# Graph attention with layer norm on one core: other row groups, the rows of p made earlier, the bins turned to a row earlier, squares on ScalarE

## The reference, cut to what matters

```
Wh, We = x @ W, ent @ W
p, q = Wh @ a1, We @ a2
e = leaky_relu(p[:, None] + q[None, :], 0.2)
e = where(adj > 0, e, -9e15)
h = softmax(e, axis=1) @ ent + x
x = x + elu(h)
out = (x - mean(x)) / sqrt(var(x) + 1e-5)      # over the 64 features
```

## Time and profile before

| | us |
|---|---|
| median of 3 runs | 375.44 (375.23 to 376.32) |
| profiled execution | 377.46 |
| its span | 375.4 |
| DVE busy | 308.4 (82%) |
| PE busy | 305.7 (81%) |
| ACT busy | 264.4 (70%) |
| POOL busy | 47.2 (13%) |

### The profile page before, as it was taken

One profiled execution on the slowest core, in us unless ns is written; L12 is line 12 of the kernel. 1 busy time (PEld: TensorE's weight loads), 2 busy tenths in 40 slices (PEclk: granted clock), 3 DMA queues, 4 the chain that ended last, 5 costly groups with the idle time before them and its releaser, 6 DMA issues.

```text
span 375.4 us, 9071 instructions
## 1 busy us (share of the span) xinstructions
PE 305.7 (81%) x3920; PEld 163.2 (43%) x3920; DVE 308.4 (82%) x436; ACT 264.4 (70%) x263; POOL 47.2 (13%) x54
## 2 busy tenths in 40 slices
PE   1379599997879999996999979879997767957750
PEld 0356466665545554552545435335442313412220
DVE  1894586863797999569899996799999999999955
ACT  1163299897588989589999975799876568646530
POOL 5012111110101001400100041000000500000201
PEclk9999879998989999998999989999999999999995
DMA  7999999999977940999665009940000000000000
GB/s 151 251 206 174 186 200 161 205 207 208 188 119 115 151 74 2 144 208 209 103 91 81 0 3 168 205 72 0 2 2 2 2 28 3 3 0 2 0 30 22
DMA packets 35240, 37.32 MB, mean 99 GB/s; under 512 B 832, under 2 KB 34432, under 8 KB 35200
## 3 DMA queue, kind: packets, MB, share of 16 engines
q0 software_dynamic: 33408, 33.56, 56.3%
q1 hardware_dynamic: 1792, 3.18, 3.0%
HBM read 69.24 MB, written 1.05 MB: 187 GB/s over the span
## 4 chain that ended last, share of the span: by engine, by line
PE 35%; DVE 27%; issue 23%; ACT 11%; DMA 2%; POOL 1%; POOLq 0%; DVEq 0%; SPq 0%; ACTq 0%
PE acc L744 13%; PE pairs L693 10%; DVE xm L522 8%; DVE wts L530 7%; PE acc L747 6%; ACT mask L315 5%; ACT wts L329 3%; PE hist L709 3%; DMA ent_sb<-ent_blocks_dram 2%; DVE y L563 1%; PE misc L668 1%; ACT drow L340 1%; DVE ent_part L615 1%; PE misc L724 1%; POOL rstd L272 1%
## 5 line engine op out<-in xcount | busy, mean ns | idle before, releaser
L329 ACT ACTIVATE wts<-wts,q_bias 128x768 f32<-128x768 f32 (+2 forms) x160 | 152.1, 976 | 56.1 <-DVE wts L530 55.9
L744 PE MATMUL acc<-wts,ent_sb 128*32 128x384 f32 (+2 forms) x1280 | 152.5, 525 | 28.3 <-ACT wts L329 19.4
L530 DVE SCALAR_TENSOR_TENSOR wts<-pb,q_bend,xm 128x768 f32<-128x768 f32 (+2 forms) x160 | 167.5, 1070 | 8.2 <-PE acc L747 7.7
L315 ACT ACTIVATE mask<-pairs 128x2048 bf16<-128x2048 bf16 (+2 forms) x67 | 104.3, 1559 | 35.8 <-PE pairs L693 35.5
L747 PE MATMUL acc<-wts,onesf 128*32 128x256 f32 (+1 forms) x1152 | 93.2, 362 | 0.0
L522 DVE TENSOR_TENSOR xm<-mask,drow 128x1536 bf16<-128x1536 bf16 (+2 forms) x80 | 80.8, 1010 | 9.9 <-ACT drow L340 9.9
L693 PE MATMUL pairs<-ident,raw 128*128 128x128 bf16 x1024 | 79.5, 235 | 1.8 <-ACT mask L315 0.9
L693 PEld LDWEIGHTS pairs<-ident,raw 128*128 128x128 bf16 x1024 | 65.2, 106 | 27.9 <-issue 27.5
L747 PEld LDWEIGHTS acc<-wts,onesf 128*32 128x32 f32 x1152 | 41.7, 112 | 71.3 <-issue 66.0
L744 PEld LDWEIGHTS acc<-wts,ent_sb 128*32 128x32 f32 x1280 | 34.7, 109 | 57.7 <-ACT wts L329 43.3
L266 POOL DMA_DIRECT2D raw<-adj_dram x40 | 33.4, 836 | 153.9 <-PE pairs L693 151.3
(11 more groups left out here) (99 smaller groups left out, 107.8 us busy)
## 6 DMA issues: line engine op xcount, KB each, us to landing
raw<-adj_dram POOLq DMA_DIRECT2D x16, 1024.0 KB, 12.2
raw<-adj_dram POOLq DMA_DIRECT2D x16, 768.0 KB, 10.6
raw<-adj_dram POOLq DMA_DIRECT2D x8, 512.0 KB, 10.2
ent_sb<-ent_blocks_dram SPq DMA_DIRECT2D x1, 1024.0 KB, 7.5
x_sb<-x_dram SPq DMA_DIRECT2D x2, 256.0 KB, 8.4
out_dram<-y SPq DMA_DIRECT2D x2, 256.0 KB, 2.0
x_sb<-x_dram SPq DMA_DIRECT2D x2, 192.0 KB, 8.2
out_dram<-y SPq DMA_DIRECT2D x2, 192.0 KB, 4.6
```

Source lines behind the costliest of these rows:

```text
L315: act.activation(mask[:, i % RING:i % RING + 2, 0:n], pairs[j % 2][:, :, 0:n], ACT.Relu, scale=2.0 ** LIFT).then_inc(act_mask_done, 1)
L329: act.activation(part, part, ACT.Exp, bias=q_bias[:, b:b + 1]).then_inc(w_done, 1)
L530: dve.scalar_tensor_tensor(wts[:, i % SLOTS, 0:n], pb[:, P * TILE0[g]:P * TILE0[g] + n], q_bend[:, b:b + 1], xm[:, i % XS, 0:n], ALU.max, ...
L744: pe.matmul(acc[0][to:to + Q, 0:n], ent_sb[:, b, Q * f:Q * f + Q], part[:, n * k:n * k + n], start=(b == 0), stop=(b == NB - 1))
```

## The change

- `SIZES` becomes 6, 8, 8, 8, 2.
- All eight pieces of pb are made during the first group's turning, one ahead of each of the pairs 8 to 15, on PE and on ACT. The pieces at the steps of group 0 are gone, with their waits. The first spreading of the bins and the first `masked` wait for all eight.
- DVE finds the shift (`find_shift`) before it sums the entities (`ent_part`, line 615), PE's small product for the highest p stands one pair later, and DVE takes its first mask at pair 9 and not 7.
- Bins to row: at b = 22 PE completes the bins of the next group, ACT copies them at 23 (was 24), PE spreads them at 24 (was 27), PE makes the row at 27 (was 30), and ACT takes it at 28 (was 30), ahead of the masks of that step. DVE decodes at 27 as before. In each step PE's `weigh` now stands before the spreading and the row, and in step 2 of a group the last `weigh` of the old group stands before the pair.
- Parts of `finish`: ACT's exponential reads y itself, and the minimum with 1 is taken in the addition that follows, so DVE's separate minimum goes. The squares are taken by ACT (`squares`, at b = 22) in place of DVE. Part numbers and steps move accordingly; there are 11 parts. For the last group, too, DVE waits for ACT's exponential and squares.
- The power of group g on POOL stands behind a later load (for groups 0 and 1, 4 chunks later).
- DVE takes other pairs of groups 1 and 2 for its masks: of group 2 pairs 2 and 5 in place of 4, 9 and 14.

The constants are as the diff has them. The diff, with context lines left out:

```diff
@@ -5,7 +5,7 @@
 N, M, F = 4096, 4096, 64
-SIZES = (4, 6, 8, 8, 6)
+SIZES = (6, 8, 8, 8, 2)
...
@@ -36,20 +36,24 @@
 HIST_LAG = 3
+HIST_END = 22
 ACC_AT = 2
-TURN_SUMS_AT = 6
+TURN_SUMS_AT = 5
 TURN_BACK_AT = 10
-ELU_AT = 18
-HIST_COPY_AT = 24
-SPREAD_AT = 27
+ELU_AT = 15
+SQUARE_AT = 22
+HIST_COPY_AT = 23
+SPREAD_AT = 24
 DECODE_AT = 27
-ROW_AT = 30
-DROW_AT = 30
-FINISH_AT = {8: 0, 13: 1, 14: 2, 15: 3, 16: 4, 20: 5, 21: 6, 22: 7, 23: 8, 24: 9, 25: 10, 29: 11}
-P_ROWS_AT = range(2, 23, 3)
+ROW_AT = 27
+DROW_AT = 28
+FINISH_AT = {7: 0, 12: 1, 13: 2, 14: 3, 18: 4, 19: 5, 20: 6, 21: 7, 25: 8, 26: 9, 30: 10}
+ROWS = N // 512
+ROWS_FROM = 8
...
@@ -236,7 +242,7 @@
             g, k = divmod(j, GROUP_PAIRS)
-            return g == 0 and k >= 7 and k % 2 == 1 or g == 1 and k % 3 == 2 or g == 2 and k % 5 == 4
+            return g == 0 and k >= 9 and k % 2 == 1 or g == 1 and k % 3 == 2 or g == 2 and k in (2, 5)
...
@@ -288,7 +294,7 @@
                 load(n)
-                if n == NB // CHUNK * (deviations + 1) + (24 + RING) // CHUNK + 1:
+                if n == (NB * (deviations + 1) + 28 + RING) // CHUNK + RAWS - 1:
...
@@ -329,9 +335,14 @@
             def elu(g):
-                e_g = e[:, 0:SIZES[g], :]
+                n = SIZES[g]
                 act.wait_ge(att_done, g + 1)
-                act.activation(e_g, e_g, ACT.Exp).then_inc(elu_done, 1)
+                act.activation(e[:, 0:n, :], y[:, 0:n, :], ACT.Exp).then_inc(elu_done, 1)
+
+            def squares(g):
+                n = SIZES[g]
+                act.wait_ge(centred, g + 1)
+                act.activation(e[:, 0:n, :], y[:, 0:n, :], ACT.Square).then_inc(square_done, 1)
...
@@ -354,9 +365,9 @@
             for j in range(4, GROUP_PAIRS):
+                if j >= ROWS_FROM:
+                    p_row(j - ROWS_FROM)
                 store_pair(j)
-                if j == 10:
-                    p_row(0)
...
@@ -365,19 +376,20 @@
                         take_acc(g - 1)
+                    if g + 1 < NG and b == DROW_AT:
+                        take_row(g + 1)
...
                         store_pair(j)
-                    if g == 0 and b in P_ROWS_AT:
-                        p_row(1 + P_ROWS_AT.index(b))
...
                         elu(g - 1)
+                    if g and b == SQUARE_AT:
+                        squares(g - 1)
...
                         copy_hist(g + 1)
-                    if g + 1 < NG and b == DROW_AT:
-                        take_row(g + 1)
...
             elu(NG - 1)
+            squares(NG - 1)
...
@@ -578,31 +590,28 @@
                     fin_wait()
-                    fin_inc(dve.tensor_tensor(y_g, y_g, x_gr, ALU.add))
+                    dve.tensor_tensor(y_g, y_g, x_gr, ALU.add).then_inc(att_done, 1)
                 elif part == 4:
-                    fin_wait()
-                    dve.tensor_scalar(e_g, y_g, 0.0, None, ALU.min).then_inc(att_done, 1)
+                    dve.wait_ge(att_done, g + 1)
+                    dve.wait_ge(elu_done, g + 1)
...
                     fin_wait()
-                    dve.wait_ge(elu_done, g + 1)
-                    fin_inc(dve.scalar_tensor_tensor(y_g, e_g, -1.0, y_g, ALU.add, ALU.add))
+                    fin_inc(dve.scalar_tensor_tensor(y_g, e_g, 1.0, y_g, ALU.min, ALU.add))
...
                     fin_wait()
-                    fin_inc(dve.scalar_tensor_tensor(y_g, spread(mean), -1.0 / F, y_g, ALU.mult, ALU.add))
+                    dve.scalar_tensor_tensor(y_g, spread(mean), -1.0 / F, y_g, ALU.mult, ALU.add).then_inc(centred, 1)
                 elif part == 8:
-                    fin_wait()
-                    fin_inc(dve.tensor_tensor(e_g, y_g, y_g, ALU.mult))
+                    dve.wait_ge(square_done, g + 1)
+                    fin_inc(dve.tensor_reduce(var[:, 0:n], e_g, AX.X, ALU.add))
                 elif part == 9:
-                    fin_wait()
-                    fin_inc(dve.tensor_reduce(var[:, 0:n], e_g, AX.X, ALU.add))
-                elif part == 10:
...
                 else:
+                    dve.wait_ge(centred, g + 1)
...
@@ -611,13 +620,13 @@
             p_highest()
+            find_shift()
...
             dve.tensor_reduce(ent_part[:, :], ent_sb[:, :, :].rearrange("p b f -> p f b"), AX.X, ALU.add).then_inc(part_done, 1)
-            find_shift()
...
             decode(0)
-            dve.wait_ge(p_rows, 1)
+            dve.wait_ge(p_rows, ROWS)
...
@@ -632,10 +641,8 @@
                     if b % 2 == 0 and s + 2 < STEPS:
-                        if b == NB - 2:
-                            dve.wait_ge(p_rows, 8)
                         masked(s // 2 + 1)
-            for part in range(12):
+            for part in range(11):
...
@@ -660,8 +667,6 @@
                     pe.wait_ge(shift_step, 2)
-                if c == 1:
-                    pe.wait_ge(sum_done, 1)
...
@@ -715,9 +720,9 @@
                     pe.wait_ge(shift_step, 3)
-                    pe.wait_ge(p_rows, 1)
+                    pe.wait_ge(p_rows, ROWS)
                 if g == 1:
-                    pe.wait_ge(p_rows, 8)
+                    pe.wait_ge(sum_done, 1)
...
@@ -783,13 +788,13 @@
             for j in range(GROUP_PAIRS):
+                if j >= ROWS_FROM:
+                    p_row(j - ROWS_FROM)
                 turn_pair(j)
-                if j == 5:
+                if j == 6:
...
                     p_to_all()
-                if j == 9:
-                    p_row(0)
...
@@ -799,21 +804,21 @@
                     s = NB * g + b
+                    if g and b == LAG - 1:
+                        weigh(g - 1, NB - 1)
...
                         turn_pair(j)
-                    hist_to(made_by(s - HIST_LAG))
-                    if g == 0 and b in P_ROWS_AT:
-                        p_row(1 + P_ROWS_AT.index(b))
+                    hist_to(min(made_by(s), GROUP_PAIRS * (g + 2)) if b == HIST_END else made_by(s - HIST_LAG))
...
                         turn_back(g - 1)
+                    if s >= LAG and not (g and b == LAG - 1):
+                        weigh(*divmod(s - LAG, NB))
...
                         make_row(g + 1)
-                    if s >= LAG:
-                        weigh(*divmod(s - LAG, NB))
...
```

More of the change, by code:

```diff
@@ L205, in attention_layernorm @@
         rstd_done = sem("rstd_done")
+        centred = sem("centred")
+        square_done = sem("square_done")
         y_done = sem("y_done")
```

## The result

The changed kernel takes 353.7 us against 375.5 us: the ratio is 0.941, with a 95% interval of 0.939 to 0.944. That is 21.8 us less, where 7.8 were forecast, and it lies outside the range of 362 to 377. The profiled execution has a span of 350.7 us, and took 1.1 us less than the median; the one of the kernel before took 2.0 us more than its median.

The account below looks back on a forecast made before the run. The bound changes by stage: PE in group 0, three engines near full in groups 1 and 2, DVE in groups 3 and 4. New stages 55.3 + 69.5 + 70.1 + 67.5 + 65.9 + 28.0 + 11.3 = 367.6 us; range 362 to 377.

Parts of the forecast that it names:

- my step from span to median: Whole kernel: median 375.44 stood at the span 375.4 before, so the predicted span of 367.6 was taken as the median.
- 5.5 off the old group 2: New group 1: DVE's waits for decode (3.5) and drow (some 2.4) vanish, taken as 5.5 with PE's slow stretch included.
- larger pairs: Group 1, PE: six pairs larger by 2 tiles, 6 x 0.33 = 2.0 us more.
- ACT's queue: Group 1: ACT has 63.1 + 3.2 us of busy time in a stage of 70, so 1.0 is added.
- PE's plain sum of 64.1: Group 0, PE: 32 steps at 1.08 and 22 pairs of 8 at 1.34 us make 64.1.
- slow start: Group 0, PE: slow after the decode gap, 2.5 us, as in the kernel before.
- uneven pairs: Group 0, PE: pairs fall unevenly, four in five steps, costing 1.7 us.
- two cycles slow and six fast: Before the weights, PE: pair, piece and bins take 3.0 us slow, 1.7 fast; pairs 8 to 15 make 16.2, 7.5 more.
- rival A: Before the weights: pieces of pb keep PE slow, 26.4 instead of 16.2 us, +10.2 to 377.8; chance 0.12.
- my 166: Group 0, DMA: 11.5 MB in 69.5 us is 166 GB/s against 193 before; costed at nothing, 2 us if PE gets faster.
- Pairs 8 to 15 took 8.7 us (31.8 to 40.5): Before the weights, PE in the kernel before: the base from which 16.2 us for these pairs was counted as 7.5 more.
- Rival D: Squares on ACT need another table set: two loads of 1.28 us in each of five groups, +12.8 to 380.4; chance 0.03.

Follow-up runs that it names:

- b_early: Kernel before with the new order from bins to row, but without the two moves of `weigh`: 360.4 us, ratio 0.958.

## Why the prediction was wrong, step by step

**Where the 13.9 us lie.** 367.6 was forecast and the median is 353.7. Against the span of 350.7 the stages miss 16.9: 2.2 before the weights, 5.7 in group 0, 4.2 in group 1, 0.2, 1.6 and 1.0 in groups 2 to 4, and 2.0 in the tail. The other way, 3.0, goes my step from span to median: I set the median equal to the span, since the profiled execution before lay 2.0 above its median, but the median after is 3.0 above the span shown.

**Groups 0 and 1: what I added on top was mis-sized, and this is the main error, 9.9 of the 16.9 us.** The mechanism was right. The copy ahead of the masks, the early spreading and the early row did what the rows said, and the waits are gone. Their price was nearly right as well, where I set one: 5.5 off the old group 2, and the order alone took 6.0 off it. The old groups 0 and 1, which lost 7.5 and 8.5, I never priced, since the forecast put other stages in their place. The step that failed is what I added beside this in those new stages: 5.4 us in group 0, of which the stage shows nothing (next paragraph), and 3.0 in group 1, which cost 0.5. For group 1 I took 73.4 - 5.5 (waits) - 0.8 (finish) + 2.0 (larger pairs) + 1.0 (ACT's queue) = 70.1. With everything but the sizes the old group 2 takes 65.4, which is 6.0 for the order and 2.0 for the rest, where I had 0.8; and with the new sizes the stage takes 65.9, so that larger pairs and ACT's queue cost 0.5 and not 3.0. These three differences, 0.5, 1.2 and 2.5, make up the 4.2. They are read from single profiles.

**Group 0: 69.5 forecast, 63.8 measured.** PE's plain sum of 64.1 was right. On top I put 5.4 (spreading and row, slow start, uneven pairs), and the stage doesn't have it. The slow start did come: from 52.5 to 58.2 the granted clock is 0.53, 32 transposes take 3.62 us, where later pairs of 16 take 1.07 each, and the first `weigh` 1.51 against 0.85. But the stages are cut at DVE's exponents, and DVE runs up to five slots ahead. When group 1's first exponents begin at 116.9, PE still has some four steps of group 0 to weigh, at 1.08 each. The timeline of PE, the slow start, a `weigh` at the full rate, the last two of group 0 and the first of group 1:

```profile
52.56 3.62 PE L698 MATMUL pairs<-ident,raw 128*128 128x128 bf16 x32
56.10 1.51 PE L749 MATMUL acc<-wts,ent_sb 128*32 128x384 f32 x8
...
118.87 0.85 PE L749 MATMUL acc<-wts,ent_sb 128*32 128x384 f32 x8
...
120.12 0.89 PE L749 MATMUL acc<-wts,ent_sb 128*32 128x384 f32 x7
121.20 0.89 PE L749 MATMUL acc<-wts,ent_sb 128*32 128x384 f32 x7
...
123.67 1.03 PE L749 MATMUL acc<-wts,ent_sb 128*32 128x512 f32 x8
```

Group 1's first weigh, of 512 columns, begins at 123.67, 6.8 us behind DVE, where group 0's began 3.0 behind (56.10 against 53.10). By PE's own clock group 0 takes 67.6, 3.5 over the plain sum, so 3.8 us of its bill go to later stages. I priced each stage as if it were closed; that overlap is what I had left out. Group 1's plain pitch is 3.93 us for two steps and a pair of 8:

```profile
133.61 1.07 PE L698 MATMUL pairs<-ident,raw 128*128 128x128 bf16 x16
...
137.54 1.07 PE L698 MATMUL pairs<-ident,raw 128*128 128x128 bf16 x16
```

16 x 3.93 = 62.9. The other 3.0 of the 65.9 are what is left for spreading, rows and turned sums, which I didn't add up, and for what is carried in and out.

**Before the weights: 55.3 forecast, 53.1 measured, but by another bound.** I had PE's pairs and pieces there, two cycles slow and six fast, and DMA nowhere in this stage. PE was fast for all eight (12 transposes in 0.84), and it waited for adj. The timeline of PE, and the longest piece of the chain of waits in this stretch:

```profile
39.04 0.84 PE L698 MATMUL pairs<-ident,raw 128*128 128x128 bf16 x12 [0.22 <-DMA raw<-adj_dram]
...
42.84 0.84 PE L698 MATMUL pairs<-ident,raw 128*128 128x128 bf16 x12 [0.22 <-DMA raw<-adj_dram]
```

```profile
26.28 16.52 DMA raw<-adj_dram
```

A chunk of 768 KB comes every 3.80 us and holds two pairs; PE needs 3.4 for two pairs and two pieces, by my terms. So the pieces of pb were free here: with six of them moved away the first stage was no shorter (54.0 against 53.1), and the pair that waits for the last load began at 42.70 there and at 42.84 here. My rival A (PE stays slow) did not happen. I costed the DMA for group 0 only. No wait of PE for it stands there, but it moved 202 GB/s, close to the 205 of the first stage and well over my 166, so it had little room left.

My base for this stage was also misread. "Pairs 8 to 15 took 8.7 us (31.8 to 40.5)" leaves out two pairs. The timeline of PE before, with pairs 8 and 9 and the piece of pb behind them:

```profile
28.80 1.03 PE L693 MATMUL pairs<-ident,raw 128*128 128x128 bf16 x8
...
31.04 1.01 PE L693 MATMUL pairs<-ident,raw 128*128 128x128 bf16 x8 [0.87 <-DVE mask L511]
31.84 1.06 PE L668 MATMUL misc<-identf,pcol 128*128 128x128 f32 x4
```

Pairs 8 to 15 took 11.7 us, from 28.8. With that my own terms give 52.3 for the stage and not 55.3. It would have been nearer to the 53.1, by luck, since PE wasn't the bound.

**Groups 2 to 4 and the tail.** Group 2 is within 0.2, group 4 within 1.0: the 1.13 for two steps of 2 tiles held. DVE is idle for 2.0 us in group 4, where I gave 4.1 for waits, and busy for 25.1, where I had 23.9, so a part of that closeness is luck. Group 3 is 1.6 below, which I didn't take apart. With the squares back on DVE groups 1 to 4 are longer by 0.6, 1.2, 0.7 and 0.7, and the median by 2.8: the 0.7 that I gave groups 2 to 4, and the full group 1 pays as well. The rule of the Trainium skill that I weighed (ScalarE: Activation LUTs, Rules for kernel authors: multiplications on VectorE) would have made this kernel slower. Rival D didn't come: the trace after has a single ACT_TABLE_LOAD. The Trainium skill (ScalarE: Activation LUTs, Table sets: the hidden batching unit) has it so for cheap functions, but doesn't name the square among them; the 2.66 us for a switch stand in its section What ACT_TABLE_LOAD costs, and no run here has a switch to show them. The tail is 2.0 below the forecast: DVE idles for 0.45, 0.38 and 0.88 us for the exponential, the squares and the power, where I had given 0.55 twice and had taken nothing off the 1.44 for the power of 6 tiles; and the last step, the copies and the feature rows are 2.7 shorter, where I had 2.1. The rest I didn't take apart. The timeline of DVE in the tail:

```profile
345.44 0.29 DVE L597 SCALAR_TENSOR_TENSOR y<-y,x_sb 128x128 f32<-128x128 f32 x1 [0.45 <-ACT e L340]
...
347.08 0.29 DVE L609 TENSOR_REDUCE var<-e 128x2 f32<-128x128 f32 x1 [0.38 <-ACT e L345]
...
348.45 0.29 DVE L616 TENSOR_TENSOR y<-y,rstd 128x128 f32<-128x128 f32 x1 [0.88 <-POOL rstd L278]
```

**The sizes.** The forecast never set them against the old ones. It took each new stage from the nearest old stage and so held them for a gain by the way. Undone on one chip they prove to be a loss of 5.1 us, in a change that wins 21.8.

**Sum of the parts.** The order alone saves 21.8; the sizes on top cost 7.8; the pieces of pb, the squares and the rest (minimum, choice of masks, POOL's place) save about 8.0, of which 3.3 and 2.8 were measured each by itself, by undoing it in the changed kernel. The rest of about 2 was not taken apart. The parts depend on each other: the order is worth 13.9 when it is undone last, and the sizes cost 5.1.

## What to carry to other kernels

Price a stage by the plain sum of its busiest engine, taken from two rows of undisturbed pitch, and be sparing with what is put on top: an engine that may lag behind by several slots can pass it on to a later stage that has room. The visible waits at the ends of groups were no bad price for their removal here, 21.3 us against 22.0 gained, provided that none comes up elsewhere, as in b_early. Put a small piece for which another engine waits at a step where nothing long stands ahead of it, and let the consumer's next slot be freed before it. And a moved tile is paid for in every stage that handles it, the one that loads and turns it as well as the one that uses it: try its place against the old one before it goes in with other edits.

## What the runs showed of the hardware

PE's half rate followed a gap ahead of it. In the kernel with six pieces of pb moved back, a gap of 2.12 us at 29.4 was followed by one pair at 0.84 and the next at 1.49 us (granted clock 0.50 from 33.3 to 34.9), and a gap of 1.63 us by pairs at 1.28 and 1.46; in the changed kernel, where a piece of pb lies in the same wait for DMA, the gap is 1.30 us and the pair behind the next piece takes 0.83 (granted clock 1.00 from 26 to 40). The timelines of PE, of the first and of the second:

```profile
31.49 0.84 PE L702 MATMUL pairs<-ident,raw 128*128 128x128 bf16 x12 [2.12 <-DMA raw<-adj_dram]
...
33.34 1.49 PE L702 MATMUL pairs<-ident,raw 128*128 128x128 bf16 x12
...
42.70 1.28 PE L702 MATMUL pairs<-ident,raw 128*128 128x128 bf16 x12 [1.63 <-DMA raw<-adj_dram]
```

```profile
31.57 0.84 PE L698 MATMUL pairs<-ident,raw 128*128 128x128 bf16 x12 [1.30 <-DMA raw<-adj_dram]
...
33.11 0.83 PE L698 MATMUL pairs<-ident,raw 128*128 128x128 bf16 x12
```

Where work filled the wait for DMA, the rate stayed up. These are one profile each; that the filling is the cause was not tried by itself.
